# A mixture-of-experts sandwich: the mixer's last four steps with centring on TensorE, squares summed on ScalarE, and the routing one step later

## The reference, cut to what matters

```python
x = L0_attn_x                                     # (16, 256, 128), float32
x = x + _layernorm(mixer(_layernorm(x)))          # mixer, over time within each of 16 sequences:
#   it = sigmoid(x @ Wi.T + bi); rt = sigmoid(x @ Wr.T + br)
#   at = exp(-8 * softplus(cap_lambda) * rt); gx = sqrt(1 - at**2) * (it * x)
#   h[t] = at[t] * h[t-1] + gx[t]
x = x + _layernorm(experts(_layernorm(x)))        # 32 experts, the best 4 of each row
#   scores = sigmoid(x @ gate_w.T); the 4 largest of scores + e_bias, weights scores / their sum
#   out = sum over the 4 of weight * ((silu(x @ w1[e]) * (x @ w3[e])) @ w2[e])
```

## Time and profile before

| | |
|---|---|
| median of 3 runs | 340.8 us (339.17, 340.8, 340.84) |
| profiled execution, from its first to its last instruction | 340.3 us |
| mixer, to the first block of half 0 | until 113.8 us |
| slots of half 0, of half 1 | until about 181 us, until about 243 us |
| dense pass, then the last norm | until about 323 us, until the end |
| busy in the span: PE, DVE, ACT, POOL | 83%, 75%, 64%, 69% |

### The profile page before, as it was taken

The page is one execution under the profiler, slowest core; times in us unless marked ns, Lnnn a source line. Parts: engine busy times, 40 slices in busy tenths (PEclk is TensorE's granted clock), DMA queues, the critical chain, the costliest instruction groups (busy, mean ns, idle before and its releaser), DMA issues.

```text
span 340.3 us, 6589 instructions
## 1 busy us (share of the span) xinstructions
PE 281.3 (83%) x1515; PEld 223.4 (66%) x1516; DVE 256.6 (75%) x976; ACT 217.5 (64%) x546; POOL 235.1 (69%) x272
## 2 busy tenths in 40 slices
PE   4575675697585899999997999999999999999950
PEld 2243252553443798889886999889776766899720
DVE  3778689778989577787447989644578987977796
ACT  6938766888773565555553656555588678865752
POOL 4396777777777777777741777777777777777710
PEclk9965679565876599999999999999999999999995
DMA  4999999961111556667746899876521111421232
GB/s 104 323 309 287 281 279 282 305 158 47 52 51 47 149 156 195 190 192 211 214 146 181 232 268 267 239 215 181 156 56 46 48 53 48 130 72 54 64 94 62
DMA packets 84000, 54.81 MB, mean 161 GB/s; under 512 B 8033, under 2 KB 80513, under 8 KB 83969
## 3 DMA queue, kind: packets, MB, share of 16 engines
q1 hardware_dynamic: 57472, 30.85, 33.3%
q0 software_dynamic: 6912, 14.17, 14.1%
q10 hardware_dynamic: 19584, 9.44, 9.8%
HBM read 25.07 MB, written 29.36 MB: 160 GB/s over the span
## 4 chain that ended last, share of the span: by engine, by line
PE 63%; DVE 16%; ACT 11%; issue 5%; DMA 2%; SPq 1%; ACTq 0%; DVEq 0%
PE bank L1616 13%; PE bank L1648 9%; PE bank L1681 7%; PE bank L1692 7%; PE bank L1686 7%; PE bank L1629 5%; PE bank L1611 4%; PE bank L1484 3%; PE bank L1517 3%; DVE st L744 1%; ACT hn L472 1%; ACT L570 1%; ACT L482 1%; ACT xn2T L539 1%; DMA xb<-xs_dram 1%
## 5 line engine op out<-in xcount | busy, mean ns | idle before, releaser
L435 POOL DMA_INDIRECT yk<-ys_dram,row_ys x108 | 106.5, 986 | 42.7 <-issue 26.2
L426 POOL DMA_INDIRECT xs_dram<-xn_all,row_xs x108 | 108.5, 1004 | 36.2 <-issue 32.6
L1616 PE MATMUL bank<-w,xbT 128*128 x288 | 60.4, 333 | 1.3 <-ACT xbT L639 1.2
L1114 DVE TENSOR_TENSOR act_a<-silu,bank 128x192 f32<-128x192 f32 x72 | 25.4, 352 | 29.7 <-ACT silu L642 26.6
L1616 PEld LDWEIGHTS bank<-w,xbT 128*128 128x128 f32 x288 | 46.0, 193 | 2.3 <-issue 2.1
L639 ACT COPY xbT<-bank 128x256 f32<-128x256 f32 x72 | 26.8, 373 | 31.6 <-PE bank L1611 28.6
L1648 PE MATMUL bank<-w2s,aT 96*128 x288 | 45.6, 280 | 0.1
L1648 PEld LDWEIGHTS bank<-w2s,aT 96*128 96x128 f32 x288 | 37.7, 191 | 2.0 <-issue 1.6
L1692 PE MATMUL bank<-at_at,xn_all 128*128 128x384 f32 (+1 forms) x96 | 34.5, 441 | 3.4 <-DVE at_at L1373 3.3
L642 ACT ACTIVATE silu<-bank 128x192 f32<-128x192 f32 x72 | 23.9, 332 | 20.0 <-PE bank L1616 19.1
L1123 DVE COPY yb<-bank 128x256 f32<-128x256 f32 x72 | 30.3, 421 | 7.3 <-PE bank L1648 6.9
(11 more groups left out here) (216 smaller groups left out, 531.6 us busy)
## 6 DMA issues: line engine op xcount, KB each, us to landing
xb<-xs_dram SPq DMA_DIRECT2D x144, 64.0 KB
ys_dram<-yb ACTq DMA_DIRECT2D x72, 128.0 KB
xs_dram<-zeros SPq DMA_DIRECT2D x2, 2048.0 KB, 15.1
ys_dram<-zeros SPq DMA_DIRECT2D x1, 2816.0 KB, 13.5
ys_dram<-zeros SPq DMA_DIRECT2D x1, 2560.0 KB, 17.9
x_sb<-in_L_attn_x_dram SPq DMA_DIRECT2D x8, 256.0 KB, 5.2
xs_dram<-xn_all,row_xs POOLq DMA_INDIRECT x108
yk<-ys_dram,row_ys POOLq DMA_INDIRECT x108, 2.5
```

The source lines that it names most:

```text
L426: pool.indirect_dma_start(out=xs[h], out_offset=bass.IndirectOffsetOnAxis(ap=row_xs[:, j, k:k + 1], axis=0), in_=xn2_all[:, j, :], in_offs ...
L435: pool.indirect_dma_start(out=yk[h][:, j - h * TP, k, :], out_offset=None, in_=ys[h], in_offset=bass.IndirectOffsetOnAxis(ap=row_ys[:, j, ...
L1616: ins = pe.matmul(ps_gu[o][:, b * 2 * I:(b + 1) * 2 * I].rearrange("t (w a i) -> t w a i", w=2, a=1), xbT[:, o, b, :], w13[:, :, bass.ds(e ...
```

## The change

Steps 2 and 3 of the mixer stay as they are, apart from `std_1` of group 2 and the second gate matmul of group 4, which move across the border between step 3 and step 4. From step 4 on, a `dense_step` takes the place of `step` on three engines.

- The recurrence's output of groups 3 to 6 is turned by a matmul with `cen` (the unit matrix less 1/128 everywhere), which gives rows with their mean taken off. GpSimd makes `cen` once at the start.
- ScalarE squares these rows with a sum along them (`squares_h`) and takes the square root of the mean (`std_h`); VectorE's statistics, the shift and ScalarE's `norm_h` go. VectorE multiplies by the reciprocal and adds the residual in one operation from PSUM (`join_h`).
- The square root of the second norm (`std_1`) comes a step later (group d = s - 2), and its reciprocal, norm, `turn_1` and `logits` with it, which puts them later in the step in which they were; the score, the choice and the rows come a step later (group e = s - 3). `gate_i` of a group is issued on TensorE a step ahead, beside `gate_r`.
- The choices of groups 5, 6 and 7, of which two stood in the slots of half 0, all stand there now, and `turn_1` and `logits` of group 6 too. The filler transposes `keep_on` go from the steps 4 to 7.

```diff
+        DENSE = 4
+        CENTRED = range(DENSE - 1, G - 1)
+        cen, sumh = sb("cen", [P, P]), sb("sumh", [P, GT])
...
+            pool.tensor_scalar(cen[:], ident[:], -1.0 / C, None, ALU.add).then_inc(s_const, 1)
...
+                if g in CENTRED:
+                    act.wait_ge(a_hn, GT * (g + 1))
+                    act.activation(stdh[:], sumh[:], ACT.Sqrt, bias=eps_c[:], scale=1.0 / C).then_inc(a_stdh, 1)
+                else:
+                    act.wait_ge(v_varh, normed(g) + 1)
+                    act.activation(stdh[:], mvh[:, :, 1], ACT.Sqrt, bias=eps_c[:]).then_inc(a_stdh, 1)
+
+            def squares_h(g):
+
+                act.wait_ge(pe_h, g + 1)
+                act.wait_ge(v_x1, GT * g)
+                for j in range(GT):
+                    act.activation(hn[:, j, :], ps_h[:, j * P:(j + 1) * P], ACT.Square,
+                                   accum_out=sumh[:, j:j + 1]).then_inc(a_hn, 1)
...
-                if real(c):
+                if real(c) and a < DENSE:
                     std_1(c)
...
+            def dense_step(s):
+                a, b, c, d, e = s + 1, s, s - 1, s - 2, s - 3
+                gate_r(b)
+                gate_i(b)
+                if s > DENSE:
+                    score(e)
+                factor(b)
+                act.preload_act_table(ACT.Sqrt)
+                if real(a):
+                    turned_x(a)
+                std_1(d)
+                root(b)
+                squares_h(c)
+                std_h(c)
+                turned_1(d)
+                if a + 1 in BY_ACT:
+                    norm_x(a + 1)
+                if real(a):
+                    act.preload_act_table(ACT.Tanh)
+
             def last():
...
+            def join_h(g):
+
+                dve.wait_ge(v_rstdh, g + 1)
+                for j in range(GT):
+                    dve.scalar_tensor_tensor(out=tile(g * GT + j), in0=ps_h[:, j * P:(j + 1) * P], scalar=rstdh[:, j:j + 1],
+                                             in1=tile(g * GT + j), op0=ALU.mult, op1=ALU.add).then_inc(v_x1, 1)
...
+            def dense_step(s):
+                b, c, d, e = s, s - 1, s - 2, s - 3
+                gate(b)
+                if s > DENSE:
+                    best(e)
+                square(b)
+                if s == G - 1:
+                    tables(0, 1)
+                if s > DENSE:
+                    take_out(e)
+                inverse_1(d)
+                if s > DENSE:
+                    chosen(e)
+                norm_1(d)
+                weight_in(b)
+                if s > DENSE:
+                    rows(e)
+                    if routed(e) < GT:
+                        scores_of(e)
+                inverse_h(c)
+                if s == G - 1:
+                    tables(0, 2)
+                scan(b)
+                join_h(c)
+                if s < G - 1:
+                    stats_1(c)
+                    if s > DENSE:
+                        rows_cast(e)
+                    spread_1(c)
+                else:
+                    rows_cast(e)
+
             def last():
...
+                    if g in CENTRED:
+                        ins = pe.matmul(ps_h[:, j * P:(j + 1) * P], hT[:, j * P:(j + 1) * P], cen[:], start=True, stop=True)
+                    else:
+                        ins = pe.transpose(ps_h[:, j * P:(j + 1) * P], hT[:, j * P:(j + 1) * P], ident[:])
...
+            def dense_step(s):
+                a, b, d, e = s + 1, s, s - 2, s - 3
+                if real(a):
+                    turn_x(a)
+                    gate_r(a)
+                else:
+                    tables(0, 1)
+                if s > DENSE:
+                    positions(e)
+                if s == G - 1:
+                    tables(0, 2)
+                turn_1(d)
+                if real(a):
+                    gate_i(a)
+                logits(d)
+                turn_h(b)
...
+                elif t == 0:
+                    best(G - 3)
                 elif t == 1:
+                    take_out(G - 3)
+                    chosen(G - 3)
+                elif t == 2:
+                    packed_rows(0, 0)
+                elif t == 3:
                     best(G - 2)
-                elif t == 2:
+                elif t == 4:
                     take_out(G - 2)
-                elif t == 3:
                     chosen(G - 2)
...
+                if h == 0 and isinstance(t, int) and t == 0:
+                    turn_1(G - 2)
```

More of the change, by code:

```diff
@@ L259, in routed, with normed @@
             return TH[half(g)] - (GH - 1) * GT if g % GH == GH - 1 else GT
+        def normed(g):
+            return sum(n not in CENTRED for n in range(g))
         def by_act(g):
@@ L614, in _ @@
             second()
-            for s in range(2, G):
+            for s in range(2, DENSE):
                 step(s)
+            for s in range(DENSE, G):
+                dense_step(s)
             last()
@@ L916, in step @@
                     gate(b)
-                if real(e) and e < G - 1:
+                if real(e):
                     best(e)
@@ L925, in step @@
                     weight_in(b)
-                if real(e) and e < G - 1:
+                if real(e):
                     rows(e)
-                    if e + 1 not in LATE:
+                    if e < 2:
                         rows_cast(e)
-                    if routed(e) < GT:
-                        scores_of(e)
                 if real(b):
@@ L937, in step @@
                     spread_1(c)
-            def last():
+            def dense_step(s):
[29 more added lines that the diff above has]
+                    rows_cast(e)
+            def last():
+                stats_h(G - 1)
+                spread_h(G - 1)
+                stats_1(G - 2)
+                spread_1(G - 2)
+                inverse_h(G - 1)
+                shift_h(G - 1)
                 inverse_1(G - 2)
                 norm_1(G - 2)
-                inverse_h(G - 1)
-                shift_h(G - 1)
-                rows_cast(G - 3)
                 by_tile(G - 1)
@@ L1097, in _ @@
             second()
-            for s in range(2, G):
+            for s in range(2, DENSE):
                 step(s)
[L1100 to L1104, removed]
+            for s in range(DENSE, G):
+                dense_step(s)
+                if s == G - 2:
+                    tables(0, 0)
             last()
@@ L1171, in ahead @@
             def ahead(t):
-                if t in (5, 7):
-                    rows(G - 2 + (t - 5) // 2)
+                if t in (3, 5, 7):
+                    rows(G - 3 + (t - 3) // 2)
                 if t in (9, 11, 13):
@@ L1576, in _ @@
             second()
-            for s in range(2, G):
+            for s in range(2, DENSE):
                 step(s)
-                if s > GH:
-                    tables(0, s - GH - 1)
-            last()
+            for s in range(DENSE, G):
+                dense_step(s)
+                if s == G - 2:
+                    tables(0, 0)
             def ahead(t):
-                if t in (5, 7):
-                    positions(G - 2 + (t - 5) // 2)
+                if t in (3, 5, 7):
+                    positions(G - 3 + (t - 3) // 2)
                 if t in (9, 11, 13):
```

59 lines of the change are left out of this document (30 added, 29 removed).

## The result

The changed kernel takes 343.55 us (median of 9 runs, 341.64 to 345.39) against 341.36 for the kernel before (9 runs, 339.17 to 342.51). The ratio is 1.0057, with an interval of 1.0035 to 1.0079: between 1.2 and 2.7 us slower, where 1.0 us faster was forecast and 343.3 was the range's upper end. Measured later beside other kernels the ratio was 1.0083 [1.0055, 1.0111].

What follows compares the result with a forecast made beforehand. Half 1's start was held by GpSimd's 108 unbroken scatters, with half 0's tail close by. Scatters end 2.5 later less 0.5, yet `act_a`'s first turn comes 1.2 earlier; less 0.2 for clock, -1.0: 339.8 us, range 337.3 to 343.3.

Steps and rivals of the forecast that it cites:

- Step 4's start: Mixer, ScalarE: with the square root moved to the next step, step 4's first tanh comes at 56.23, 3.1 us earlier.
- The step's length: Mixer: a step's length becomes ScalarE's, so step 4 takes 10.24 us against 12.25 before.
- The squares: ScalarE in the mixer: eight squares with a sum cost 0.6 us more on the path, between nothing and 3.7.
- The break in the scatters: GpSimd before its 33rd scatter: group 2's rows come late and stop the scatters for 2.5 us, between 0 and 5.6.
- My 0.7 from plain rows: Group 2's first scatter, summed from profile rows without additions: 77.6, which is 0.7 us behind the earlier 76.93.
- The relief from the joins: GpSimd's scatters: joins reading one operand in PSUM disturb them less, 0.5 us back, between nothing and three times 0.5.
- the hand-over between the halves: TensorE between half 0 and half 1: idles some 3 us; the lower clock at half 1's first slots costs 0.2 us.
- My 7.1 from the scatters' end to the first turn of `act_a`: Start of half 1: 1.96 until its loads start, 2.6 until they land, 2.5 to the first turn.
- Everything behind half 1's start moves with it: Half 1 and after: the same work on TensorE, shifted as a whole with half 1's start, no extra cost.
- the rivals: Three other outcomes: no break in the scatters (337.8 us, chance 0.29), a long break (0.17), a second break (0.09).
- a long break: Rival: group 2's rows stop GpSimd's scatters over 5.2 us; with 6.5, 3.0 slower, 343.8 us; chance 0.17.
- the second break: Rival: group 5's rows, now in slot 5 of half 0, also stop the scatters, 2.5 us; 342.3 us; chance 0.09.

Runs made afterwards that it cites:

- e2: Changed kernel plus twelve filler transposes on TensorE between the halves (eight before half 1's first block, four before the second); ratio 1.0012 to the kernel before.
- e1: Changed kernel with the cast of a group's rows directly behind the rows instead of at the step's end; ratio 1.0013 to the kernel before.
- e4: Changed kernel with the edits of e1 and e2 together (early cast, twelve fillers); ratio 0.9985 to the kernel before.
- e5: e4 with the four loads of w2p two steps of SyncE's loop later; ratio 0.9994 to the kernel before.
- e6: e4 with GpSimd's first gathers of half 0 held until the first output of half 1 is done; ratio 1.0025 to the kernel before.
- e9: e4 with group 5's row cast in slot 4 of half 0 instead of slot 5; ratio 0.9970 to the kernel before.
- after: The changed kernel as first measured, no further edit; 343.55 us, ratio 1.0057 to the kernel before; its profiled execution 341.64 us.
- e0: The changed kernel once more, unedited, as the yardstick of its group; 344.52 us, ratio 1.0083 to the kernel before.
- e3: Changed kernel with the four 384 KB loads of w2p two steps of SyncE's loop later; ratio 1.0118 to the kernel before.
- e4_again: The kernel of e4 measured once more; ratio 0.9974 to the kernel before.
- e9_again: The kernel of e9 measured once more; ratio 0.9958 to the kernel before.
- e7: Kernel before, SyncE's first loads of half 1 held until half 0's last output block is copied, so TensorE idles; ratios 1.0082 and 1.0107 to the kernel before.
- e10: e8_before_idle_warm with GpSimd's gathers of half 0 held until the twelfth output of half 1; the run took 362.91 us.
- e7_before_idle: First run of the e7 kernel (kernel before, half 1's first loads held); one run of it was 347.1 us.
- e8_before_idle_warm: e7 plus twenty filler transposes on TensorE in the idle stretch (sixteen before half 1's first block, four before the second); ratio 1.0143 to the kernel before.
- e8_again: The kernel of e8_before_idle_warm measured once more; ratio 1.0117 to the kernel before.

## Why the prediction was wrong

- Step 4's start was right: 56.23 forecast, 54.91 + 1.42 = 56.33 measured. The step's length was right: 10.24 forecast, 10.64 measured, then 11.34 and 9.22.
- The squares were costed at +0.6 and bring a gain: the four and their sums run from 59.73 to 60.87, 1.14 us, where the four `hn` took 1.51.
- The break in the scatters had the right place and cause, where it came, and too large a size: 2.5 forecast; 1.03, 0, 1.72 and 0 in the four profiles with the late cast. My 0.7 from plain rows was nearer than what I put on top.
- The relief from the joins (0.5) is not there: a scatter takes 1001, 1009, 1002 and 1012 ns on the mean in those four profiles, 1004 before. The adds went, but the scans stayed, which read two tiles in SBUF as well. In each of the eleven profiles of the changed mixer one scatter, issued within 0.3 us of the start of the last step's scan, takes 1.76 to 2.04 and ends 0.76 to 0.78 behind that scan's end, while no scatter behind the first takes more than 1.50 in the seven of the old mixer. e2's timelines of GpSimd and VectorE show the longest: 2.04 beside a scan of 1.25, 1.08 more than its neighbours. The trace agrees there with the rule cited from the Trainium skill (SBUF — State Buffer, "Who interferes with whom"), with nearly the scan's full length lost. Over all 108 scatters the mean does not move.

```profile
97.31 2.04 POOL L433 DMA_INDIRECT xs_dram<-xn_all,row_xs  x1 [0.30 <-issue]
```

```profile
97.33 1.25 DVE L946 TENSOR_TENSOR_SCAN hT<-at_at,gx 128x256 f32<-128x256 f32 x2
```

- The two terms together were +2.0 on the scatters. The four late-cast profiles have 141.76, 141.62, 142.61 and 141.95, a mean of 141.99; the seven with the early cast (e1, e4, e5, e6, e9) 140.73. So the late cast costs 1.3 us against the early one, and 0.9 against the seven profiles of the old mixer (mean 141.04, before's 141.07 among them).
- **The step that failed is the hand-over between the halves**, in the prediction's words "for a lower clock at half 1's first slots I add 0.2". No row stood behind that 0.2. I let TensorE idle for some 3 us; the idle time was right (1.66 + 0.97 in two waits) and the price was not. The cold profiles (after, e0, e1, e3) have hand-overs of 10.97, 11.39, 10.37 and 11.03, a mean of 10.94; the warm ones (e2, e4_cast_warm, e4_again, e5, e6, e9_cast4_warm; e9_again is left out, since half 0's tail ended last there) 9.18. That is 1.8 us for the clock. Counted from half 1's first transposes to the second turn, without what comes ahead of them, it is 7.24 against 5.18. My 7.1 from the scatters' end to the first turn of `act_a` holds for no cold profile (9.0 to 9.4), and the warm ones have 7.6 to 8.3. So a part of the miss is not the clock: the sum lets the first blocks land together, and in the warm profiles TensorE waits for blocks again behind the first one, 0.2 to 1.2 us in all ahead of the first turn.
- The balance of the changed kernel's profile, counted from the first scatter: the scatters cost 1.3 less than forecast (+0.7 for +2.0), the way to the first turn 1.7 more (9.0 for 7.3, the 0.2 included), the rest of half 1 1.6 more (nothing was forecast). Two errors worked against each other; had the break been as long as I made it, the forecast would have missed by another 1.3. That is luck, not a better part of the sum.
- "Everything behind half 1's start moves with it" failed for the second slots, which still ran at the lower clock (1.93 from the first turn to the second, 1.13 before). Behind them it is not shown to have failed. From the second turn of `act_a` to the dense pass it took 56.57 before and 57.4 to 58.9 in the changed kernel, e1, e2 and e3, with waits for blocks of 0.55 to 1.94 us in four of these five profiles (after, e0, e1, e2; none in e3, which has 57.44). But the 56.57 is the lowest of the old mixer's values, which are 57.0 to 58.0 in the three profiles of e7, so most of the ranges overlap. The dense pass did move with it.
- Of the rivals none was the right one. The price of 343.8 came about, but not by a long break; the second break showed only where the first was mended (0.37 in e1 and in e5).
- The start of half 0 (110.1 forecast, 106.71 + 1.42 = 108.1 measured) and its longer slots (69.7 us from its first transposes to its end, 67.4 before) were of no account: half 0 ended at 176.41, and half 1's first block came 1.66 us later.

What stays open: the medians differ by 2.2 us and by 2.8, the profiles counted from the first scatter by 1.0 and 1.8. The rest is in executions of which there is no trace. Their mean clock gives a hint: of the changed kernel's nine, the three fastest (341.6 to 342.3) have 0.898 to 0.907, the three slowest (344.3 to 345.4) 0.883 to 0.888, an order that e0's seven show less and the executions of the kernel before at 340 to 345 us do not show. Where in them the clock was low is not known. And what exactly stands in front of a late block in half 1 is only partly shown: gathers by e10, not the loads of `w2p` by e3 and e5.

## What to carry to other kernels

When a change frees an engine ahead of a floor that it does not move (here 108 scatters in a row), the time can become idle time of the engine behind the floor, as TensorE's did here. Ask at which clock that engine comes back, price it from a row at the lower level, and look whether a few fillers in the wait give it back. And where a chain of transfers is the floor, put what feeds it first in every step: the cast belonged directly behind its rows.

## What the hardware showed that I had not expected

- TensorE idle for 1.66 and then 0.97 us between the halves came back at a granted clock of 0.50 for some 5 us, and so it did in the kernel before (2.80 and 0.60 in e7_before_idle); twelve transposes in that time held it at 1.00. A wait of 1.60 in the middle of half 1 did the same in e8_before_idle_warm, as its windows of 6 and of 2 us show:

```profile
209.70:215.70 6.00, 5.63 (x29) 0.72 1.04 237
...
212.00:214.00 2.00, 2.00 (x9) 0.50 1.13 183
```

Not each wait did: behind one of 1.01 in e8_again (at 210.65), and behind one of 1.71 that followed eight fillers in e4_again (at 179.23), the clock stayed at 1.00.

- A square with a sum on ScalarE is an ACTIVATE of 0.27 us and an ACTIVATION_READ_ACCUMULATOR of 0.20 to 0.23; the pair repeats every 0.25 us, faster than an Identity with scale and bias of the same shape (0.35).
- With the first slots of half 1 faster, TensorE lost the time again in waits for `xb` (e8): DMA shares of 0.99 to 1.04 from 192 to 216 us stand beside them in the first profile.
